# Attention with a fused layer norm and FP4 feed-forward: who copies a head's outputs, and where one block of scores stands

## What is computed

```python
h = _layernorm(x) * (1 + ca) + sa
q, k, v = einsum(h, query_proj), einsum(h, key_proj), einsum(h, value_proj)
sim = jnp.einsum('bnkh,bmhk->bnhm', q, k)
attn = softmax(sim / 4, axis=1)               # over the query tokens n, for each key m
o = jnp.einsum('bnhm,bmhv->bnhv', attn, v)
x = x + ga * jnp.einsum('bnhv,dhv->bnd', o, output_proj)
h = _layernorm(x) * (1 + cb) + sb
x = x + gb * ffn(h)                           # gate, up, silu, down; operands in blockwise FP4
```

## Time and profile before

| | |
|---|---|
| median of 3 runs | 1684.09 us (1681.34 to 1684.48) |
| the profiled execution | 1685.73 us |
| its span, first to last instruction | 1684.4 us |
| from one head's copy to the next, in the attention part | 37.00 us |
| busy share PE / DVE / ACT / POOL | 97% / 94% / 82% / 46% |
| mean granted TensorE clock | 0.996 of 2.4 GHz |

### The profile page before, as it was taken

How to read it: one execution, slowest core, us unless ns; L and a number is a source line. 1 busy time by engine, 2 the same in 40 slices (tenths; PEclk the granted TensorE clock), 3 DMA queues, 4 the chain that set the end, 5 groups by cost and what they waited for, 6 DMA issues and landing times.

```text
span 1684.4 us, 38849 instructions
## 1 busy us (share of the span) xinstructions
PE 1640.7 (97%) x15454; PEld 817.2 (49%) x15454; DVE 1578.9 (94%) x1705; ACT 1374.7 (82%) x2508; POOL 779.4 (46%) x1625
## 2 busy tenths in 40 slices
PE   9999999999999999999999999999999999999998
PEld 8743333333333333673333333333333379999997
DVE  7899999999999999769999999999999879888887
ACT  5599999999999999569999999999999833333332
POOL 3034445444444545303454544566654457555542
PEclk8999999999999999999999999999999999999999
DMA  6102111112111112511111121111112533534420
GB/s 232 65 9 72 51 49 46 45 50 67 52 51 51 46 45 76 168 38 45 46 45 45 45 70 50 52 51 46 46 45 64 157 113 126 155 125 155 145 67 19
DMA packets 83110, 123.15 MB, mean 73 GB/s; under 512 B 4713, under 2 KB 69105, under 8 KB 82929
## 3 DMA queue, kind: packets, MB, share of 16 engines
q1 hardware_dynamic: 82512, 120.15, 22.5%
q10 hardware_dynamic: 416, 0.53, 0.1%
HBM read 74.52 MB, written 46.15 MB: 72 GB/s over the span
## 4 chain that ended last, share of the span: by engine, by line
DVE 64%; PE 32%; issue 2%; ACT 1%; POOL 1%; DMA 0%; POOLq 0%; DVEq 0%
DVE nm L1073 60%; PE acc L447 13%; PE slot L447 10%; PE acc L615 6%; PE slot L671 1%; PE slot L586 1%; DVE ost L1086 1%; ACT e_sb L825 1%; PE slot L468 0%; PE acc L646 0%; DVE qs L1140 0%; DMA v_sb<-in_x 0%; DVE e_sb L1128 0%; DVE e_sb L1147 0%; PE slot L494 0%
## 5 line engine op out<-in xcount | busy, mean ns | idle before, releaser
L1073 DVE TENSOR_REDUCE nm<-slot 128x1 f32<-128x1024 f32 x1024 | 1166.1, 1213 | 20.2 <-PE slot L586 18.0
L825 ACT ACTIVATE e_sb<-slot,nm 128x1024 f32<-128x1024 f32 x1024 | 1137.6, 1113 | 17.5 <-DVE nm L1073 12.5
L615 PE MATMUL acc<-e_sb,vp 64*64 64x512 f32 x8192 | 1060.7, 594 | 6.3 <-DVE ost L1086 4.7
L586 PE MATMUL slot<-stq,stk 64*64 64x512 f16 x4096 | 411.6, 388 | 21.6 <-ACT e_sb L825 21.6
L586 PEld LDWEIGHTS slot<-stq,stk 64*64 64x64 f16 x4096 | 117.6, 103 | 626.5 <-ACT e_sb L825 592.7
L615 PEld LDWEIGHTS acc<-e_sb,vp 64*64 64x64 f32 x8192 | 283.3, 132 | 188.1 <-issue 73.8
L1309 POOL TENSOR_TENSOR dlt<-nm 128x4 f32<-128x4 f32 x128 | 25.8, 202 | 408.2 <-DVE nm L1073 408.2
L825 ACT ACTIVATION_READ_ACCUMULATOR e_sb<-slot,nm 128x1 f32 x1024 | 199.8, 195 | 0.0
L1300 POOL TENSOR_TENSOR vp<-v_sb,fac 128x512 f32<-128x512 f32 x128 | 133.6, 1044 | 10.2 <-POOL fac L1290 0.3
L1286 POOL TENSOR_TENSOR rtot<-tot,mone 128x4 f32<-128x4 f32 x128 | 132.8, 1038 | 10.0
L1280 POOL TENSOR_TENSOR wsum<-cor,ssum 128x8 f32<-128x8 f32 x128 | 26.0, 203 | 233.7 <-ACT cor L855 233.7
(11 more groups left out here) (180 smaller groups left out, 1931.5 us busy)
## 6 DMA issues: line engine op xcount, KB each, us to landing
o_r<-o_heads SPq DMA_DIRECT2D x32, 1024.0 KB, 7.2
stk<-qk_parts SPq DMA_DIRECT2D x128, 128.0 KB
o_heads<-ost_hi SPq DMA_DIRECT2D x64, 256.0 KB, 3.4
o_heads<-ost SPq DMA_DIRECT2D x64, 256.0 KB, 4.1
v_sb<-in_x SPq DMA_DIRECT2D x16, 512.0 KB, 6.1
qk_parts<-e_sb SPq DMA_DIRECT2D x32, 256.0 KB, 2.3
stq<-qk_parts SPq DMA_DIRECT2D x128, 64.0 KB
out<-e_sb SPq DMA_DIRECT2D x32, 128.0 KB, 1.8
```

The source lines that it names most:

```text
L586: mm = pe.matmul(slot[s][side * VD:(side + 1) * VD, c * 512:(c + 1) * 512], stk[c * 64:c * 64 + 64, h % 2, i * P + side * VD:i * P + (side ...
L615: mm = pe.matmul(acc[half * VD:(half + 1) * VD, c * 512:(c + 1) * 512], vp[rows, g % 3, gi, half, :], e_v[rows, j % ERING, n0:n0 + 512], s ...
L825: act.activation(e_v[:, j % ERING, half * 1024:(half + 1) * 1024], slot[u % 3][:, :], ACT.Exp, bias=nm[:, g % 4, i, half:half + 1], accum_ ...
L1073: dve.tensor_reduce(nm[:, g % 4, i, half:half + 1], slot[u % 3][:, :], AX.X, ALU.max, negate=True).then_inc(maxed.sem)
```

## The change

Three things are edited. DVE copies only columns 0:256 of `acc`. ACT copies 512:1024 as before and then, after a wait for `took_low`, columns 256:512 in a second instruction, and signals `took_high` behind that one. The waits that guarded columns up to 512 by `took_low` (`take_quarter` at the start of the second batch, `project(3)` at the end) now use `took_high`. And S(J+1).0 moves on PE from behind V1 to between V0 and V1.

```diff
@@ take_quarter
             elif b:
-                pe.wait_ge(*(took_low if q == 2 else took_high).past(b * H - 1))
+                pe.wait_ge(*took_high.past(b * H - 1))
@@ project
             elif i == 3:
-                pe.wait_ge(*took_low.past(B * H - 1))
+                pe.wait_ge(*took_high.past(B * H - 1))
@@ tensor_program
                     begins = jv > 0 and jv % NT == 0
+                    begun = jv > 1 and jv % NT == 1
                     for half in range(2):
-                        if j < JT:
+                        if j < JT and not (begun and half == 0):
                             scores(b, j, half)
                         if jv >= 0 and not begins:
                             attend(b, 2 * jv + half)
                     if begins:
                         attend(b, 2 * jv)
+                        if j + 1 < JT:
+                            scores(b, j + 1, 0)
                         attend(b, 2 * jv + 1)
@@ attend_act
-                        act.copy(ost[:, 512:1024], acc[:, 512:1024]).then_inc(took_high.sem)
+                        act.copy(ost[:, 512:1024], acc[:, 512:1024])
+                        act.wait_ge(*took_low.past(b * H + h))
+                        act.copy(ost[:, 256:512], acc[:, 256:512]).then_inc(took_high.sem)
@@ attend_dve
-                    dve.tensor_copy(ost[:, 0:512], acc[:, 0:512]).then_inc(took_low.sem)
+                    dve.tensor_copy(ost[:, 0:256], acc[:, 0:256]).then_inc(took_low.sem)
```

## The result

The changed kernel takes 1702.61 us (median of 4 runs, 1700.49 to 1703.75), against 1684.28 us for the kernel before beside it: 18.3 us more, a ratio of 1.0107 with a 95% interval of 1.0095 to 1.0119. The forecast was 1703.0.

The account below looks back on a forecast made before the run. DVE bounds a head's long run and PE its boundary, where the start of max(J+1).1 decides. 30 boundaries at 0.63 us give 18.9 us, added to the median 1684.09 for 1703.0 us; range 1691.0 to 1708.0.

Parts of the forecast that it names:

- V0 late by 0.25 through ACT's second copy: At a head boundary, V0 waits for ACT's second copy, ending at 172.86, and starts 0.25 us later than before.
- S(J+1).0 waits for exp(J-1).1: On PE after V0, the moved scores need that exponential and start at 174.01; PE stands still for 0.14 us.
- The pause between V1 and V2: On PE, with no scores between them, V2 waits for V1 to complete, 0.29 us more than V1's 0.86.
- The sum: At each of 30 boundaries max(J+1).1 starts 0.63 us late: 0.25 from late `took_high`, 0.38 from the order; 18.9 us.
- The gain that was on offer: On DVE at a boundary, the shorter copy would allow max(J+1).1 at 175.66 instead of 176.11, 0.45 us earlier.
- The chain: At a boundary: max(J-1).0, exp(J-1).0, two ACT copies, V0; one DVE gap of about 1.1 us, before max(J+1).1.
- A miss without effect: ACT stands 0.8 us before exp(J+1).0, waiting for V2; PE does not need that exponential until 2 us later.
- The ends of the batches: At a batch's end ACT's idle time (0.25 us first, 2.73 second) hides the second copy; otherwise 0.3 us, twice.

Follow-up runs that it names:

- both less: Kernel before, with DVE and ACT each copying only 256 columns behind every head but a batch's first; 1676.93 us, ratio 0.9962.
- ACT mid-head: Kernel before, with one more ACT copy of 256 columns from SBUF to a spare tile mid-head in 30 heads; 1683.89 us, ratio 0.9998.

## Why the prediction was right, point by point

- **V0 late by 0.25 through ACT's second copy.** Right, 0.03 short. ACT's second copy starts 0.47 behind the first, as taken, and holds ACT 0.26 (170.30 to 170.56). It lasts 0.38 instead of 0.37, and V0 starts 0.15 behind its end instead of 0.13: 1.09 behind DVE's copy, where 1.06 was forecast.
- **S(J+1).0 waits for exp(J-1).1.** Right: 171.84 is 1.01 after V0 (1.02 forecast), where V0 takes PE 0.88; the exponential's read-out ended at 171.79.
- **The pause between V1 and V2.** 1.13 from V1's start to V2's (172.08 to 173.21), 1.15 forecast: a pause of 0.27. By the Trainium skill, TensorE: Matmul & The Clock Gate, section Single matmul latency, an estimated 0.17 was to be expected. The trace has 0.1 more; how much of the pause is the end of V1's products, the semaphore or the load of V2's weights, which waited too, is open.
- **The sum.** From DVE's copy to max(J+1).1 it was to be 176.74 - 171.93 = 4.81 us, and it is 174.56 - 169.74 = 4.82. A head is 37.63 us, 0.63 longer, 30 times, as the sum had it. The terms were off by 0.03 at most, and not all to one side (V0 0.03 later, V2's pause 0.02 shorter), so a little of the agreement to 0.01 is luck. That the parts add was shown by the runs of each alone. Against the profiled execution the sum was 1704.6, and that execution took 1700.49; the 4.1 us lie outside of the stretch between the copies and are told in the last section.
- **The gain that was on offer.** DVE's 0.45 us did not come; the run in which DVE only copies less shows that they cannot come while V0 starts where it does.
- **The chain.** V0 waits for ACT's copy by 0.43 (0.4 forecast), and DVE has its one gap before max(J+1).1, 1.00 as the row counts it (1.1 forecast from starts). What I had not forecast is that the chain leaves DVE in the long run as well; that this is no new bound shows in the long run's 32.81 us, as before.
- **A miss without effect.** ACT was to stand 0.8 us before exp(J+1).0; it stands 0.45. I had counted from the end of DVE's maximum, from which it is 0.88 (174.43 - 173.55), but ACT was itself behind by then.
- **The ends of the batches** were to cost nothing, and they did not. From the last copy of the first batch to the first of the second it is 110.69 us in both kernels, and the 18.9 us between the first and the last copy (1241.9 - 1223.0) are the 30 boundaries. At the end of the second batch, PE's first matmul behind the last chunk starts at 1357.66 and ACT's cast of L743 at 1361.12, 3.46 us later; in the changed kernel it is 3.45 (1373.86 to 1377.31).

## What to carry to other kernels

Where three engines pass work round, look for the one start from which the busy stretch runs without a gap, and price every edit by what it does to that start: here 0.27 us less on the engine with most of the chain gave nothing, and a second copy on an engine with room made V0 0.28 us late and cost nearly all of it. The chain's shares by engine can mislead there; the distance from one head's copy to the next does not. When two engines release a third together, only the later one counts, so giving work from one to the other pays only if the other was early; and before an item is moved between two others, look whether it was covering a wait between them. The same split was a gain once the whole boundary was moved to where its later end did no harm.

## What was not expected of the hardware

Two profiled executions of these kernels differ by some 4 us outside of the attention part, where nothing was changed. These are the stretches 0 to 40 us and 1358 to 1400 us of the kernel before, by engine busy us and count, then the granted clock, the share of the DMA engines and GB/s:

```profile
0.00:40.00 40.00, 37.84 (x188) 33.49 (x189) 28.60 (x85) 23.91 (x35) 13.86 (x25) 0.87 0.66 226
1358.00:1400.00 42.00, 38.41 (x274) 37.66 (x273) 33.71 (x54) 14.40 (x21) 22.41 (x38) 0.96 0.29 91
```

And the first of these stretches in the changed kernel:

```profile
0.00:40.00 40.00, 36.25 (x200) 31.35 (x201) 30.50 (x87) 25.03 (x37) 13.64 (x25) 1.00 0.73 246
```

The 0.87 is not one level. In the kernel before the clock was at 0.50, the level of 1.2 GHz, from 10 to 20 us, and at 1.00 or 0.99 in the other three quarters; the changed kernel had 1.00 in the same ten:

```profile
10.00:20.00 10.00, 10.00 (x44) 9.52 (x44) 7.74 (x29) 3.03 (x5) 2.02 (x2) 0.50 1.06 384
```
```profile
10.00:20.00 10.00, 9.13 (x64) 8.10 (x63) 8.40 (x32) 4.49 (x7) 2.02 (x2) 1.00 1.06 384
```

PE did 44 matmuls there in place of 64. In the 10 us ahead of it PE was busy for 8.34 us with 49 matmuls, and in the changed kernel, whose clock did not fall, for 8.48 with 51.

With the clock of 0.87 the first copy of a head came at 134.9 us, at 1.00 at 132.1, and the runs in which it came at 132.5 and 132.6 have a mean clock of 1.00 as well. So the spans of the two profiles differ by 14.8 us where the boundaries account for 18.9: a difference of two single executions of this kernel is good to some 4 us only, while from one boundary to the next the distance of two copies repeats to 0.01 us. In the matmuls between the copies the clock was 1.00 throughout. The transfers of those 40 us differ too (226 against 246 GB/s), so the clock goes with the later start but is not shown to be its only cause. It goes with the time of whole executions too: of those of the kernel before beside the experiments, the ones with a mean clock of 1.000 took 1681.83 to 1682.05 us, those with 0.995 took 1687.26 to 1687.57. What decides whether the clock falls was not tried.

And a copy of 256 columns on ACT took 0.363 us where it read PSUM ("both less") and 0.393 us where it read SBUF ("ACT mid-head"). The two stand at different places of a head, so the memory is not shown to be the cause.
